# Linear attention of a two-layer block: the query softmax divided at the context product, the second norm applied by ScalarE

## The reference, cut to what matters

```
xn = layer_norm(x, norm_g, norm_b)
q = softmax(xn @ Wq + bq, over the 8 features of a head)
k = softmax(xn @ Wk + bk, over the tokens)
v = xn @ Wv + bv
ctx = einsum('bnhd,bnhl->bhdl', k, v)
y = einsum('bnhd,bhdl->bnhl', q, ctx)
h = layer_norm(y, sn_g, sn_b) * (1 + scale) + shift      # scale, shift from the condition
out = x + gate * (silu(h) @ out_W + out_b)
```

## Time and profile before

| what | us |
|---|---|
| median of three runs | 243.66 |
| lowest, highest | 242.99, 245.1 |
| the profiled execution: its time, and its span | 243.22, 241.5 |
| busy in the span: PE, DVE, ACT, POOL | 198.5, 168.9, 125.1, 147.2 |

### The profile page before, as it was taken

How to read it: one execution, slowest core, us unless ns; L and a number is a source line. 1 busy time by engine, 2 the same in 40 slices (tenths; PEclk the granted TensorE clock), 3 DMA queues, 4 the chain that set the end, 5 groups by cost and what they waited for, 6 DMA issues and landing times.

```text
span 241.5 us, 5854 instructions
## 1 busy us (share of the span) xinstructions
PE 198.5 (82%) x1986; PEld 151.2 (63%) x1986; DVE 168.9 (70%) x501; ACT 125.1 (52%) x326; POOL 147.2 (61%) x358
## 2 busy tenths in 40 slices
PE   3659677399999999988987898969999589997742
PEld 3337434377777777766766576757887457785531
DVE  4799545768888888998386315358989478799631
ACT  3438122066777777766355636424343056787640
POOL 8446741396787878767875303153632267999972
PEclk9999985779999999999999979999999999999975
DMA  6860000000000000000000000000000000000112
GB/s 124 250 243 0 1 0 0 3 1 3 3 3 3 1 4 4 0 3 3 0 3 4 3 1 0 3 0 0 3 1 0 3 0 3 0 22 26 35 35 60
DMA packets 9914, 5.12 MB, mean 21 GB/s; under 512 B 3025, under 2 KB 9758, under 8 KB 9758
## 3 DMA queue, kind: packets, MB, share of 16 engines
q1 hardware_dynamic: 6494, 4.08, 5.5%
q10 hardware_dynamic: 3392, 0.68, 1.4%
HBM read 3.71 MB, written 1.05 MB: 20 GB/s over the span
## 4 chain that ended last, share of the span: by engine, by line
PE 53%; DVE 22%; POOL 12%; issue 5%; DMA 3%; ACT 2%; ACTq 1%; POOLq 0%; DVEq 0%
PE bank L1666 11%; DVE qkpad L1392 9%; PE bank L1675 7%; PE bank L1757 6%; PE bank L762 4%; PE bank L751 4%; PE bank L752 4%; PE bank L1734 4%; DMA xin<-in_x_dram 3%; PE bank L1698 3%; POOL rstd L472 2%; PE bank L737 2%; POOL qx L503 2%; POOL xs L526 2%; POOL res L514 2%
## 5 line engine op out<-in xcount | busy, mean ns | idle before, releaser
L1392 DVE TENSOR_REDUCE qkpad<-bank 128x4 f32<-128x512 f32 x64 | 41.2, 686 | 19.9 <-PE bank L1666 19.2
L1118 ACT ACTIVATE probs<-bank 128x512 f32<-128x512 f32 x64 | 34.8, 595 | 33.5 <-PE bank L1675 33.5
L1666 PE MATMUL bank<-kBD,qTs 32*128 32x256 f32 x256 | 40.4, 436 | 8.7 <-DVE modr L1342 4.3
L1675 PE MATMUL bank<-qTm,kBD 32*128 32x128 f32 x512 | 39.0, 292 | 1.1 <-ACT probs L1118 1.1
L1666 PEld LDWEIGHTS bank<-kBD,qTs 32*128 32x128 f32 x256 | 25.2, 203 | 16.0 <-DVE qkpad L1392 7.5
L1675 PEld LDWEIGHTS bank<-qTm,kBD 32*128 32x128 f32 x512 | 32.7, 194 | 2.1 <-ACT probs L1118 1.6
L984 POOL TENSOR_TENSOR partner<-qk,rope 128x96 f32<-128x96 f32 x30 | 13.5, 470 | 16.6 <-ACT qk L1163 16.6
L1698 PE MATMUL bank<-ident,qkpad 128*128 128x128 f32 x96 | 18.5, 308 | 2.4 <-DVE x L1437 2.4
L545 ACT ACTIVATE th<-bank 128x256 f32<-128x256 f32 x24 | 9.2, 384 | 19.1 <-PE bank L737 8.9
L1757 PE MATMUL bank<-probs,vpad 128*32 128x128 f32 x512 | 18.4, 285 | 0.3 <-ACT probs L1118 0.3
L1698 PEld LDWEIGHTS bank<-ident,qkpad 128*128 128x128 f32 x96 | 12.3, 157 | 9.1 <-issue 8.4
(11 more groups left out here) (234 smaller groups left out, 527.5 us busy)
## 6 DMA issues: line engine op xcount, KB each, us to landing
gate<-in_cond_dram SPq DMA_DIRECT2D x1, 1024.0 KB, 4.3
out_dram<-res SPq DMA_DIRECT2D x8, 128.0 KB, 1.8
xin<-in_x_dram ACTq DMA_DIRECT2D x2, 256.0 KB, 5.5
xin<-in_x_dram SPq DMA_DIRECT2D x1, 512.0 KB, 5.8
ada_n<-in_L_cond_ada_w_dram SPq DMA_DIRECT2D x1, 256.0 KB, 6.3
w_n<-in_L_cond_w_dram SPq DMA_DIRECT2D x2, 128.0 KB
qkv_n<-in_L_cond_qkv_w_dram SPq DMA_DIRECT2D x1, 192.0 KB, 4.7
w_n<-in_L_cond_w_dram SPq DMA_DIRECT2D x1, 170.5 KB
```

What stands on the lines that cost most here:

```text
L1118: q.activation(probs[2 * r + i][:, :, :, :].rearrange("p f a t -> p (f a t)"), bank[E_BANK[i]][:, :], ACT.Exp, scale=SCALE).then_inc(s_p, 1)
L1392: q.tensor_reduce(out_, bank[S_BANK[i]][:, :].rearrange("p (f a t) -> p f a t", f=2, a=2), X_AXIS, ALU.max, negate=True).then_inc(s_max, 1)
L1666: last = q.matmul(bank[S_BANK[i]][:, f * 2 * T:(f + 1) * 2 * T], qTs[b % 2][rows, f, :], kBD[b % NKB][rows, f, :, :].rearrange("p a t -> p ...
L1675: last = q.matmul(bank[E_BANK[i]][:, (2 * f + k) * T:(2 * f + k + 1) * T], kBD[t % NKB][rows, f, k, :], qTm[t % 2][rows, f, :], start=True ...
```

## The change

Three things change, all of them in the second layer.

- The tile qx and its instruction on GpSimd go. TensorE transposes the undivided exponentials `qe`. VectorE reads the context product from PSUM, multiplies by `qrec`, each reciprocal broadcast over 8 columns, and writes `y`, as the last instruction of its step. ScalarE's copy of y goes.
- The two wide instructions on GpSimd that centre and scale y go. In their place GpSimd makes a 128x2 tile `nmr3` (minus the mean, then times rstd, two instructions), and ScalarE writes `xs4` with two Identity activations of 128x128, with a scale and a bias for each partition.
- GpSimd's work on the statistics of y is done one of its steps earlier (unit t-4 instead of t-5), and still stands ahead of xs3(t). ScalarE's xs4(t-4) stands at the end of its step.

```
 blocks_gpsimd, loop over t:
-                u = t - 5
-                if is_unit(u - 1):
-                    g.wait_ge(d_rstd, u)
-                    g.wait_ge(d_xc, u)
-                    q.tensor_tensor(xs4[(u - 1) % 2][:, :, :], xs4[(u - 1) % 2][:, :, :], wide(rstd3, u - 1), ALU.mult).then_inc(d_xs, 1)
-                u = t - 4
-                if is_unit(u):
-                    g.wait_ge(c_qrec, u + 1)
-                    wait(g, c_qxTp, u - 1)
-                    q.tensor_tensor(qx[u % 2][:, :, :, :], qe[u % 2][:, :, :, :],
-                                    qrec[u % 2][:, :, :].unsqueeze(3).to_broadcast([128, UNIT, H, DH]), ALU.mult).then_inc(c_qx, 1)
                 u = t - 3        (qs, unchanged; then res(t - 8), unchanged)
...
-                u = t - 5
-                if is_unit(u):
+                u = t - 4
+                if is_unit(u):
+                    g.wait_ge(c_mv, u + 1)
+                    q.tensor_scalar(nmr3[:, pair(u)], mv3[:, pair(u), 0], -1.0, 0.0, ALU.mult, ALU.add)
                     std(u, c_mv, mv3, var3, d_var, rstd3, d_rstd)
+                    g.wait_ge(d_rstd, u + 1)
+                    q.tensor_tensor(nmr3[:, pair(u)], nmr3[:, pair(u)], rstd3[:, pair(u)], ALU.mult).then_inc(d_nmr, 1)
                 u = t            (xs3, unchanged)
...
-                u = t - 5
-                if is_unit(u):
-                    wait(g, d_xsT, u - 1)
-                    q.tensor_tensor(xs4[u % 2][:, :, :], y[:, pair(u), :],
-                                    mv3[:, pair(u), 0:1].to_broadcast([128, UNIT, D]), ALU.subtract).then_inc(d_xc, 1)
 blocks_scalar, end of the step:
-                u = t - 3
-                if is_unit(u):
-                    a.wait_ge(c_yp, u + 1)
-                    q.activation(y[:, pair(u), :], bank[Y_BANK][:, 0:UNIT * D].rearrange("p (u f) -> p u f", f=D),
-                                 ACT.Copy).then_inc(c_y, 1)
+                u = t - 4
+                if is_unit(u):
+                    a.wait_ge(d_nmr, u + 1)
+                    wait(a, d_xsT, u - 1)
+                    for j in range(UNIT):
+                        last = q.activation(xs4[u % 2][:, j, :], y[:, UNIT * u + j, :], ACT.Identity,
+                                            bias=nmr3[:, UNIT * u + j:UNIT * u + j + 1], scale=rstd3[:, UNIT * u + j:UNIT * u + j + 1])
+                    last.then_inc(d_xs, 1)
 blocks_vector, end of c_step:
+                u = t - 3
+                if is_unit(u):
+                    v.wait_ge(c_yp, u + 1)
+                    v.wait_ge(c_qrec, u + 1)
+                    q.tensor_tensor(y[:, pair(u), :].rearrange("p u (h d) -> p (u h) d", d=DH),
+                                    bank[Y_BANK][:, 0:UNIT * D].rearrange("p (g d) -> p g d", d=DH),
+                                    qrec[u % 2][:, :, :].rearrange("p u h -> p (u h)").unsqueeze(2).to_broadcast([128, UNIT * H, DH]),
+                                    ALU.mult).then_inc(c_y, 1)
 blocks_tensor, c_step, QT(t - 3):
-                    e.wait_ge(c_qx, u + 1)
+                    e.wait_ge(c_qe, u + 1)
                     wait(e, c_qxT, u)
-                    turned(bank[QT_BANK], lambda j: qx[u % 2][:, j, :, :].rearrange("p h d -> p (h d)"), c_qxTp)
+                    turned(bank[QT_BANK], lambda j: qe[u % 2][:, j, :, :].rearrange("p h d -> p (h d)"), c_qxTp)
```

More of the change, by code:

```diff
@@ L227, in dit_then_linear_attention @@
         qrec = two("qrec", UNIT, H)
-        qx = two("qx", UNIT, H, DH)
+        nmr3 = sb("nmr3", [128, B])
         qxT = two("qxT", UNIT, T)
@@ L348, in dit_then_linear_attention @@
         c_qrec = sem("c_qrec")
-        c_qx = sem("c_qx")
         c_qxTp = sem("c_qxTp")
@@ L362, in dit_then_linear_attention @@
         d_rstd = sem("d_rstd")
-        d_xc = sem("d_xc")
+        d_nmr = sem("d_nmr")
         d_xs = sem("d_xs")
@@ L585, in blocks_scalar @@
                     wait(a, c_qsum, u - 1)
-                    wait(a, c_qx, u - 1)
+                    wait(a, c_qxTp, u - 1)
                     q.activation(qe[u % 2][:, :, :, :].rearrange("p u h d -> p (u h d)"),
@@ L654, in c_step @@
                     v.wait_ge(c_qsum, u + 1)
-                    wait(v, c_qx, u - 1)
+                    wait(v, c_y, u - 1)
                     q.reciprocal(qrec[u % 2][:, :, :].rearrange("p u h -> p (u h)"),
```

## The result

The changed kernel is slower: 255.62 us, median of 4 runs (253.07 to 257.72), against 244.32 us (242.99 to 245.1, 4 runs) before; the ratio is 1.0433, 95% interval 1.0332 to 1.0535. The prediction had 250.9 with a range up to 254.0: the right side, and too little. The profiled execution, the shortest of the four, took 253.07 us, where my sum had 250.4.

A forecast was written before the change was run, and what follows sets the result against it. Bound: chain of waits through GpSimd, by a small margin. 202.31 + 5.56 + 17.43 + 5.10 + 4.91 + 5.67 puts XD(7) at 240.98, 7.2 us later; profiled 250.4, plus 0.44 gives 250.9 us, range 247.6 to 254.0.

The forecast's parts named there:

- the ring: Second-layer loop within each step: ctx, bn_aggr, GpSimd's statistics, xs3, XC, back to ctx; 5.56 by PE, 5.81 by DVE.
- first ring: Step 4, bn_aggr to bn_aggr, before hs exists: the PE branch is the longer, 5.56 us.
- three rings: Steps 5, 6 and 7, along the DVE branch: 3 x 5.81 = 17.43 us.
- steps 8 and 9: Without xs3, qs still behind the statistics: 5.10 us, then 4.91 with knb gone too.
- bn_aggr(6) to XD(7): Tail from the mean and variance of unit 6 to the last transpose, over ScalarE: 5.67 us.
- the clock: Rival: PE's pauses lower its clock, from step 9 on (252.4 us, 12%) or from step 5 on (256, 4%).
- The tail: From bn_aggr(6), chain over ScalarE's xs4 pairs, 0.80 each, with transposes and hT4/th4: 5.67 us to XD(7).
- The small instructions: Two new 128x2 GpSimd instructions, 0.15 each start to start; could move a step by up to 0.3 either way.
- Step 9: Step without xs3 and knb, DVE branch shortened by knb's 0.28 less its overlap: 4.91 us.
- The lock: VectorE and GpSimd block each other at a shared SBUF port; knb 0.12 shorter in the ring, where GpSimd waits.
- The relief of GpSimd: Rival: fewer wide GpSimd instructions remove PE's waits for L498 and qx, 3.4 us faster, 240.3 us; 4%.
- The rival that the loss ends with xs3: From step 8 steps run at about 3.9 us; steps 8 and 9 give back 2.2, 248.7 us; 12%.

The follow-up runs named there:

- the three runs that move only GpSimd's order: Changed kernel with xs3(t) ahead of the statistics, 249.67 us; with qs(t-2) ahead of them, 251.71 us; with statistics of unit t-5, 240.52 us.
- PE's pauses filled: Changed kernel plus spare TensorE products ahead of XC(4) to XC(7) and at the start of steps 9 to 12: 250.97 us.
- unit t-5: Changed kernel with GpSimd's statistics taken back from unit t-4 to t-5, all else as changed: 240.52 us, ratio 0.9873 to the kernel before.
- the second trace of the changed kernel: The changed kernel run again with nothing altered, for a second trace: 254.66 us, ratio 1.0507 to the kernel before.
- the kernel with qs first: Changed kernel with GpSimd making qs(t-2) ahead of the statistics of unit t-4, which still stand ahead of xs3(t): 251.71 us, ratio 1.0345.

## Why the prediction was right and wrong

The bottleneck and the ring were right, and the three runs that move only GpSimd's order show it. The median came out 4.7 us above the prediction. 2.6 of them are in the profiled execution (253.07 against 250.4), and the steps below divide these (they are short by 0.13 more, since the first bn_aggr came 0.13 earlier than before); the rest is that this execution lies 2.55 under the median, where I had added 0.44. By its steps, against the first trace after, and in the last column the trace with PE's pauses filled:

| step | predicted | measured | at full clock |
|---|---|---|---|
| first ring | 5.56 | 7.29 | 5.63 |
| three rings | 17.43 | 17.78 | 17.78 |
| steps 8 and 9 | 10.01 | 10.41 | 10.32 |
| bn_aggr(6) to XD(7) | 5.67 | 5.95 | 5.95 |
| sum | 38.67 | 41.43 | 39.68 |

- **The step that failed is the clock.** I had it as a rival, falling "from step 9 on" with 12% and "from step 5 on" with 4%, because the clock had stayed 1.00 in a window with PE busy 0.62 of 2.00 us. One such window of a busy stretch was no bound. The fall came in the very first ring, after 2.34 us of waiting; it lasts a few microseconds and costs 1.66 in the first ring (7.29 against 5.63) and 1.36 in a later one (7.29 against 5.93). I had priced a fall at 2 us a step. It strikes another number of rings in each execution. It was not a case beside mine but a term that belonged in the sum of it, and the sum had it at nothing. Of the 2.76 us by which the sum is short in the table, it is 1.75 (41.43 less 39.68). Without it, XD(7) lies 8.2 us further behind the first bn_aggr than before (39.68 against 31.46); my sum had 7.2. The other 1.0 is in the next points.
- **The tail** up to XD(7) was priced along ScalarE's list, and its last piece isn't that: xs4(7) waits for GpSimd's nmr of unit 7, the last link behind bn_aggr(7). This stretch takes 5.95 in place of 5.67, and as much with the pauses filled. Behind XD(7) the time is the same before and after, as the sum had it: 7.73 and 7.69 us, both at the lower clock.

```profile
242.68 0.88 ACT L593 ACTIVATE xs<-y,nmr,rstd 128x128 f32<-128x128 f32 x2 [0.55 <-POOL nmr L509]
```

- **The small instructions** were 0.10 short: nmr to var takes 0.25 from start to start, not 0.15 (202.27 to 202.52). The length of 0.19 was right, the overlap was not there. It makes the rings 5.93 instead of 5.81. Step 8, at full clock, took 5.16 against my 5.10.
- **Step 9** had the wrong branch. I took knb off DVE's branch and had 4.91; but then krec waits for ctx, which comes by ScalarE's hT4 and kxT, and the step takes 5.16:

```profile
237.34 0.17 DVE L670 RECIPROCAL krec<-bank 128x2 f32<-128x2 f32 x1 [0.22 <-PE bank L791]
```

- ScalarE's pair took 0.87, above the 0.80 of its neighbour. y took 0.42, as its neighbour did, and 0.33 from its start to the next, where the sum had 0.35.
- **The lock** fits what the traces show: knb takes 0.28 in every ring, where GpSimd waits. With unit t-5 it took 0.73 once, at 208.64, and ended with xs3(6) on GpSimd (208.73 for 0.61). Leaving the 0.12 in would have added 0.5 to the sum (steps 5 to 8), not the 0.6 that I gave.
- The relief of GpSimd was rightly refused as the outcome, and its price was near: with unit t-5 the layer is 2.98 us shorter than before, where I had 3.4.
- The rival that the loss ends with xs3 fell: steps 8 and 9 take 5.25 and 5.16.

What stays open is why the same pause lets the clock fall in one execution and not in the next. The wait of 2.34 us ahead of XC(4) stands in three traces of kernels with this ring: in the first the clock fell in XC itself, in the second trace of the changed kernel only behind K (K 0.60, then Y 0.88), and in the kernel with qs first not in that step at all. The length of the pause alone doesn't decide it. Open too is what the slower runs of the changed kernel (255.31 and 255.92 us beside 253.07) looked like. An execution with the start of the first trace and the layer of the second would take 253.07 + 2.65 = 255.7 us; this estimate makes a second fall in the rings the likely cause, but no trace of those runs shows it.

## What to carry to other kernels

In a pipeline written as lists in order, don't ask only what an instruction costs but how far ahead of its use it is made. A cheap instruction that waits for a late result, put in front of one that other engines need in the same step, joins all of them into a ring; moving it by one unit turned 4.3% slower into 1.3% faster. Check each moved wait for what stands behind it in its list, and if the new order makes TensorE pause some 2 us in every step, put the lower clock into the sum, here with 1.4 to 1.7 us for a fall.

## What the runs showed of the hardware

- Spare products of TensorE, whose results nobody reads, made a kernel some 4 us faster: 250.97 us against 254.66 and 255.62.
- At the lower level, the pair of products of K took 1.06 us instead of 0.60 and a transpose pair 0.61 to 0.69 instead of 0.38 to 0.44.
- After the same wait of TensorE, 2.34 us, the granted clock fell within the next transposes in one trace, only behind the next two products in a second and not in that step in a third.
- The profiled steps at full clock repeat to 0.01 us between executions (5.93, 5.92, 5.93); what varies is where the clock falls.
